# A decayed linear attention with experts: keys decayed in place on VectorE, values copied by ScalarE, TensorE's attention loop written out

## The chip, the cores and the metric

The kernel is one program on one core of a Trainium2 chip. The metric is the device time of a launch in microseconds; lower is better. Engines are called TensorE (PE in the profile), VectorE (DVE), ScalarE (ACT), GpSimd (POOL) and SyncE (SP, which here only issues DMAs).

## What is computed

x is (2, 2048, 128) in f32. It is normalised over its last axis, and the result feeds a chunked linear attention with forget gates (16 heads of 8) and a mixture of 8 experts of which expert 0 and one routed one act on each token. The sum of x and both is the output.

```python
q = silu(x @ Wq.T); k = silu(x @ Wk.T); v = x @ Wv.T
log_f = log_sigmoid(x @ Wf.T + delta)          # cumulated in a chunk: lb
def step(S, inputs):                           # one chunk, per head
    qb, kb, vb, lb = inputs
    o_inter = einsum('bhid,bhde->bhie', qb * exp(lb)[..., None], S)
    A = einsum('bhid,bhjd->bhij', qb, kb) * exp(where(mask, lb_i - lb_j, -inf))
    o_intra = einsum('bhij,bhjd->bhid', A, vb)
    kd = kb * exp(tot - lb)                    # the decayed keys
    S_new = exp(tot) * S + einsum('bhjd,bhje->bhde', kd, vb)
    return S_new, o_inter + o_intra
o = rms_norm(o) * norm_weight;  attention = o @ Wo.T
out = x + attention + sum_e gate_e * (silu(xn @ W1[e].T) * (xn @ W3[e].T)) @ W2[e].T
```

## The kernel before

The program is written by hand: each engine has its own instruction stream, in the order of the source, and semaphores (S[...]) tie them. The stages are: normalisation, projections (which leave the queries qT, the keys k2 with tokens on partitions, and the values v_sb in SBUF), the attention, expert 0 over all tokens, then 22 blocks of routed tokens. An accumulating DMA at the end of each block adds them to the output.

The attention goes over 32 chunks of 128 tokens, alternating between the two batch rows, so chunk n has buffer b = n % 2. It works in subchunks of 64 tokens. For chunk n the engines do this:

- GpSimd: qblk, the queries spread into masked blocks (L517, after the scores of chunk n-2); kd, the keys times the decays sdec (L520); the values copied into the block-shaped vblk (L525, after the attention product of chunk n-2); q_dec of chunk n-1, queries times their growth (L511); and an indirect DMA that scatters 128 normalised rows for the experts (L469).
- TensorE, in `step` (all matmuls are recorded at L983, in the helper mm): 16 matmuls for the scores 32*64 by 32x256; 4 for the state update from kd and vblk (64*128 by 64x128, L1105-1109); the second half of the exponents (118*128 by 118x512); output projection and sum of squares of chunk n-2; then, after VectorE's L896 has read the update, 4 matmuls state times q_dec and 64 of the attention product of chunk n-1; then the first half of the exponents of chunk n+1. Of 16 pairs of chunks the first four are written out, the next eight run in two passes of a loop over four pairs (attend_four), and the last four are written out again.
- ScalarE: copy of the output oT of chunk n-2 (L659), exponential of the first half (L654), square (L666), exponential of the second half (L654), result row of n-2 (L672), and for n = 2 to 18 the high part of one weight tile (L640).
- VectorE: for n = 3 to 19 the low part of one weight tile (L781), then the masked update (L896), decays times scores in two halves (L887), and two state updates (L904, L910).
- SyncE: for each chunk the transposed keys from HBM, the exponents, the growth rows (after L511 of the chunk n-2 frees the buffer), and at some chunks a 512 KB weight tile.

Ahead of the loop VectorE and ScalarE wait for all stores of the transposed keys (k_out), since their first buffers lie where those were. vblk is zeroed once by GpSimd (L498, semaphore blocks_zero).

Of the kernel before, what the change touches and what calls it, by code (L numbers as in the profile page):

```python
# [22 lines left out]
ALU = mybir.AluOpType  # L23
ACT = mybir.ActivationFunctionType
# [98 lines left out]
def build(nc, x, wqkv, wo, wrf, delta, nw, w13, w2, const, dleft, dright, out,  # L123
          k_scr, lb_scr, elb_scr, xsort):
    dleft, dright = dleft.bitcast(BF16), dright.bitcast(BF16)
    with ExitStack() as ctx:  # L126
# [128 lines left out]
        qblk = C.take([P, 2, HQ, P])  # L255
        k_now = C.take([P, 2, P])
        vblk = C.take([P, 2, HQ, HQ * (QR + HD)])
        kd = C.take([P, 2, D])
        q_dec = C.take([P, 2, P])
        ebuf = C.take([P, 2, H * SUB // 2])  # L260
        elb_now = C.take([P, 2, P])
# [193 lines left out]
        def _(pool):  # L455
# [58 lines left out]
            for n in range(NCH):  # L514
                b, c = n % 2, chunk(n // 2, n % 2)
                wait(pool, S["pe_a"], n - 1)
                pool.tensor_tensor(qblk[:, b], qT[:, c * P:(c + 1) * P].unsqueeze(1).broadcast_to([P, HQ, P]),  # L517
                                   cc("hsel").unsqueeze(2).broadcast_to([P, HQ, P]), ALU.mult).then_inc(S["pool_qb"], 1)
                wait(pool, S["pe_u"], n - 1)
                pool.tensor_tensor(kd[:, b, :].rearrange("p (h d) -> p h d", d=HD),  # L520
                                   k2[:, c, :].rearrange("p (h d) -> p h d", d=HD),
                                   sdec[:, c, :].unsqueeze(2).broadcast_to([P, H, HD]), ALU.mult
                                   ).then_inc(S["pool_kd"], 1)
                wait(pool, S["pe_av"], n - 1)
                pool.tensor_copy(v_of(slice(0, P), b), v_sb[:, c, :].rearrange("p (q h e) -> p q h e", q=HQ, h=HQ)  # L525
                                 ).then_inc(S["pool_v"], 1)
                if n:
                    grown_queries(n - 1)
                scatter(EARLY + n)
# [27 lines left out]
        def _(act):  # L557
# [85 lines left out]
            def attend(i):  # L643
                for b in range(2):
                    n = 2 * i + b
                    known = isinstance(n, int)

                    def has(k):
                        return not known or 0 <= n - k < NCH

                    def decays(half):
                        act.wait_ge(S["pe_d"], 2 * n + half + 1)
                        wait(act, S["dve_p"], 2 * n + half - 1)
                        act.activation(ebuf[:, half, :], PS[:, 0, :], ACT.Exp).then_inc(S["act_e"], 1)  # L654

                    if has(2):
                        act.wait_ge(S["pe_av"], n - 1)
                        wait(act, S["pe_w"], n - 3)
                        act.activation(oT[:, b, :].rearrange("p (s i) -> p s i", s=NS), PS[:, 5:7, 0:SUB], ACT.Copy  # L659
                                       ).then_inc(S["act_ot"], 1)  # L660
                    if has(0):
                        decays(0)
                    if has(2):
                        act.wait_ge(S["act_ot"], n - 1)
                        wait(act, S["pe_ss"], n - 3)
                        act.activation(squares[:, b, :], oT[:, b, :], ACT.Square).then_inc(S["act_sq"], 1)  # L666
                    if has(0):
                        decays(1)
                    if has(2):
                        act.wait_ge(S["pe_ss"], n - 1)  # L670
                        act.wait_ge(S[f"scattered{b}"], 16 * (i - 1) + 16)
                        act.activation(rows[:, bass.ds(chunk(i, b, 2), 1), 0:D + 1].rearrange("p o d -> p (o d)"),  # L672
                                       PS[:, 7, 0:D + 1], ACT.Copy).then_inc(S["act_attn"], 1)
                    high_w(n)
# [3 lines left out]
                act.wait_ge(S[f"k_out{v}"], 16 * (NGRP // 4))  # L678
            act.wait_ge(S["slots"], 1)
            act.wait_ge(S["blocks_known"], 1)  # L680

            def sorted_hi(n, u):
                act.wait_ge(S["xs_ps"], n + 1)
# [60 lines left out]
        def _(dve):  # L744
# [127 lines left out]
            for v in range(4):  # L872
                dve.wait_ge(S[f"k_out{v}"], 16 * (NGRP // 4))

            def attend(i):
                for b in range(2):
                    n, c = 2 * i + b, chunk(i, b)
# [28 lines left out]
                    if has(1):  # L906
# [2 lines left out]
                        dve.wait_ge(S["dve_s1"], n)  # L909
                        dve.scalar_tensor_tensor(state[:, u, 0, :], state[:, u, 1, :], dec[:, bass.ds(cu * NS + 1, 1)],  # L910
                                                 um[:, u, 1, :], ALU.mult, ALU.add).then_inc(S["dve_s0"], 1)

            for i in range(CPB):
                attend(i)
# [66 lines left out]
        def _(pe):  # L981
# [90 lines left out]
            def step(i, b):  # L1072
# [17 lines left out]
                if has(0):  # L1090
# [8 lines left out]
                                      k_now[rq, b, tok], qblk[rq, b, :, tok])  # L1099
                    last.then_inc(S["pe_a"], 1)  # L1100

                    pe.wait_ge(S["pool_kd"], n + 1)
                    pe.wait_ge(S["pool_v"], n + 1)
                    wait(pe, S["act_ot"], n - 1)
                    for s in range(NS):  # L1105
                        tok = slice(s * SUB, (s + 1) * SUB)
                        last = mm(PS[:, 5 + s, P:2 * P].rearrange("p (q h e) -> p q h e", q=HQ, h=HQ),
                                  kd[tok, b, :], v_of(tok, b))
                    last.then_inc(S["pe_u"], 1)
                    exponents(1)  # L1110
                if has(2):
# [82 lines left out]
                    pe.wait_ge(S["y_sb"], BT * n - BT)  # L1194
                down(N0 + n, u, [w2_sb[:, bass.ds(e - 1, 1), part].rearrange("p o f d -> p (o f) d") for part in range(2)])

            def attend_four(j):
                for k in range(4):
                    attend(4 * j + k)

            loop(pe, CPB // 4 - 1, attend_four)
            attend_four(CPB // 4 - 1)


            pe.wait_ge(S["act_e"], 2 * NCH)
# [79 lines left out]
```

## Time and profile before

| | us |
|---|---|
| runs, median of 3 | 376.96 |
| runs, lowest and highest | 374.95, 378.18 |
| profiled execution | 376.87 |
| its span | 375.1 |

| engine | busy us | share of the span |
|---|---|---|
| TensorE matmul | 328.8 | 88% |
| VectorE | 265.9 | 71% |
| GpSimd | 243.5 | 65% |
| ScalarE | 222.0 | 59% |

The span runs from the first to the last instruction of the profiled execution; about 1.8 us of its time lie outside. A share over the whole span mixes stages with different limits: the attention, from about 68 to 190 us, has to be read by itself. The granted TensorE clock is given as a share of 2.4 GHz, with two levels, 1.0 and 0.5. A busy TensorE is not one at its peak, since matmuls are pipelined.

### The profile page before, as it was taken

Reading aid. Unit: us, or ns where it says so; the run is one execution under the profiler, and the core shown is the slowest. Engines: PE = TensorE matmul, PEld = TensorE weight load, DVE = VectorE, ACT = ScalarE, POOL = GpSimd, SP = SyncE. Lnnn points to the kernel's source line nnn. Section 1 sums busy time; section 2 is a strip of 40 time slices with the busy share of each in tenths; the row PEclk is TensorE's granted clock in tenths of the full one; section 3 lists DMA queues with packets and bytes.
Section 4 is the critical chain, followed back from the end, with each engine's and each line's share of the span. In section 5 each row is a group of like instructions: output and inputs, shape, how many; then the busy total and the mean of one; then the engine's idle time right before and its main releaser. Section 6 shows DMA issues by size and latency. Waiting matters only on the chain.

```text
span 375.1 us, 14237 instructions
## 1 busy us (share of the span) xinstructions
PE 328.8 (88%) x5226; PEld 268.0 (71%) x5226; DVE 265.9 (71%) x577; ACT 222.0 (59%) x474; POOL 243.5 (65%) x292
## 2 busy tenths in 40 slices
PE   0778899599999989999988999999399997999970
PEld 0667765266666657777777999999299996999960
DVE  4973472255999989889837899978267775777740
ACT  1444788444666656555557777666167776777750
POOL 5423041655999989999949999900047776667773
PEclk9999999656999999999999999999699999999996
DMA  8588029411343422122242111111225445344332
GB/s 223 203 278 257 0 83 181 132 37 48 106 125 106 136 65 67 47 68 72 62 147 104 31 34 36 28 42 29 58 30 74 63 61 66 51 61 64 44 37 21
DMA packets 47505, 31.68 MB, mean 84 GB/s; under 512 B 12542, under 2 KB 45182, under 8 KB 47198
## 3 DMA queue, kind: packets, MB, share of 16 engines
q1 hardware_dynamic: 39662, 22.94, 23.3%
q0 software_dynamic: 7504, 7.95, 12.0%
q8 instruction: 35, 0.57, 0.6%
q10 hardware_dynamic: 288, 0.09, 0.1%
q14 instruction: 16, 0.13, 0.1%
HBM read 18.17 MB, written 12.79 MB: 83 GB/s over the span
## 4 chain that ended last, share of the span: by engine, by line
PE 80%; issue 5%; ACT 4%; POOL 4%; DVE 2%; POOLq 0%; DVEq 0%; ACTq 0%
PE PS L983 77%; POOL out L551 4%; PE PS L999 2%; PE PS L1150 1%; ACT C L577 1%; DVE rows L795 1%; ACT F L697 0%; POOLq L126 0%; ACT Z L589 0%; DVE C L887 0%; ACT L697 0%; ACT L628 0%; ACT L611 0%; POOL C L517 0%; ACT C L687 0%
## 5 line engine op out<-in xcount | busy, mean ns | idle before, releaser
L551 POOL DMA_INDIRECT out<-F,ids x44 | 68.3, 1552 | 56.8 <-DVE ids L920 33.9
L983 PE MATMUL PS<-C 64*32 64x64 f32 (+3 forms) x2816 | 88.6, 278 | 4.0 <-issue 3.0
L983 PEld LDWEIGHTS PS<-C 64*32 64x32 f32 (+3 forms) x2816 | 60.7, 123 | 30.9 <-issue 17.7
L930 DVE TENSOR_TENSOR F<-F,PS 128x512 f32<-128x512 f32 x76 | 51.4, 684 | 23.8 <-PE PS L983 14.8
L983 PE MATMUL PS<-C,W 128*128 128x256 f16 (+1 forms) x530 | 63.4, 277 | 3.9 <-DVE C L924 3.7
L697 ACT ACTIVATE F<-PS 128x512 f32<-128x512 f32 x76 | 45.4, 598 | 28.1 <-PE PS L983 21.1
L983 PEld LDWEIGHTS PS<-C,W 128*128 (+1 forms) x530 | 52.2, 100 | 11.6 <-issue 4.7
L654 ACT ACTIVATE C<-PS 128x512 f32<-128x512 f32 x64 | 38.2, 597 | 30.2 <-PE PS L983 23.6
L936 DVE TENSOR_TENSOR F<-F 128x512 f16<-128x512 f32 x76 | 52.4, 707 | 4.4 <-ACT F L702 1.1
L702 ACT ACTIVATE F<-F 128x512 f16<-128x512 f32 x76 | 47.3, 630 | 11.1 <-DVE F L930 8.6
L983 PE MATMUL PS<-xh,W 128*128 (+1 forms) x256 | 44.7, 273 | 1.7 <-DVE F L930 1.3
L887 DVE TENSOR_TENSOR C<-C,PS 128x512 f32<-128x512 f32 x64 | 41.4, 679 | 0.5
L517 POOL TENSOR_TENSOR C<-Z,kept_cst 128x512 f32<-128x512 f32 x32 | 33.7, 1053 | 10.8 <-ACT sdec L630 10.0
L469 POOL DMA_INDIRECT xsort<-rows,slot_i x32 | 36.0, 1126 | 5.2 <-issue 5.2
L983 PE MATMUL PS<-xl,W 128*128 (+1 forms) x128 | 34.9, 273 | 0.0
L896 DVE TENSOR_TENSOR C<-PS,kept_cst 128x256 f32<-128x256 f32 x32 | 13.4, 420 | 30.1 <-PE PS L983 30.1
L983 PE MATMUL PS<-Z,F 128*128 x528 | 33.7, 219 | 1.0 <-ACT F L711 1.0
L983 PEld LDWEIGHTS PS<-Z,F 128*128 128x128 f16 x528 | 31.5, 98 | 2.1 <-issue 1.3
L983 PE MATMUL PS<-dR,dL 118*128 118x512 bf16 x64 | 27.0, 422 | 4.3 <-ACT dec L632 3.4
L983 PEld LDWEIGHTS PS<-xh,W 128*128 128x128 f16 x256 | 25.0, 98 | 4.8 <-ACT F L697 1.5
L539 POOL TENSOR_SCALAR rows<-rows,small 128x128 f32<-128x128 f32 x32 | 25.3, 790 | 0.1
L659 ACT ACTIVATE C<-PS 128x128 f32<-128x128 f32 x32 | 8.9, 278 | 27.4 <-PE PS L983 27.4
(130 smaller groups left out, 569.7 us busy)
## 6 DMA issues: line engine op xcount, KB each, us to landing
F<-w SPq DMA_DIRECT2D x8, 512.0 KB
xsort<-C POOLq DMA_DIRECT2D x1, 2860.0 KB, 8.8
C<-xsort SPq DMA_DIRECT2D x22, 130.0 KB
x_sb<-x SPq DMA_DIRECT2D x8, 256.0 KB, 4.7
k_scr<-C SPq DMA_DIRECT2D x8, 256.0 KB, 2.5
C<-k_scr SPq DMA_DIRECT2D x32, 64.0 KB, 2.2
C<-elb_scr SPq DMA_DIRECT2D x32, 64.0 KB, 2.1
out<-x_sb SPq DMA_DIRECT2D x16, 128.0 KB, 1.8
```

What stands on the lines that cost most here:

```text
L469: pool.indirect_dma_start(xsort, bass.IndirectOffsetOnAxis(ap=slot_i[:, c:c + 1], axis=0), rows[:, c, :], None).then_inc(S[f"scattered{b}" ...
L517: pool.tensor_tensor(qblk[:, b], qT[:, c * P:(c + 1) * P].unsqueeze(1).broadcast_to([P, HQ, P]), cc("hsel").unsqueeze(2).broadcast_to([P, ...
L539: pool.tensor_scalar(attn[:, c, :], attn[:, c, :], rstd[:, c:c + 1], None, ALU.mult).then_inc(S["pool_attn"], 1)
L551: pool.indirect_dma_start(out, bass.IndirectOffsetOnAxis(ap=ids[:, k:k + 1], axis=0), ysb[:, n % 2, t, :], None, compute_op=ALU.add).then_ ...
L654: act.activation(ebuf[:, half, :], PS[:, 0, :], ACT.Exp).then_inc(S["act_e"], 1)
L697: act.activation(silu[:, half, :], PS[:, 2 + 4 * half, :], ACT.Silu, scale=1.0 / WS).then_inc(S["f_silu"], 1)
L702: act.activation(hid_hi[:, u, 2 * half:2 * half + 2, :].rearrange("p f t -> p (f t)"), silu[:, half, :], ACT.Copy).then_inc(S["f_hi"], 1)
L887: dve.tensor_tensor(pbuf[:, b, half * 512:(half + 1) * 512].rearrange("p (q x) -> p q x", q=2), ebuf[:, half, :].rearrange("p (q x) -> p q ...
L896: dve.tensor_tensor(um[:, b].rearrange("p s (h e) -> p s h e", e=HD), PS[:, 5:7, P:2 * P].rearrange("p s (h e) -> p s h e", e=HD), cc("hma ...
L930: dve.tensor_tensor(silu[:, half, :], silu[:, half, :], PS[:, 3 + 4 * half, :], ALU.mult).then_inc(S["f_h"], 1)
L936: dve.tensor_tensor(hid_lo[:, u, blocks, :].rearrange("p f t -> p (f t)"), silu[:, half, :], hid_hi[:, u, blocks, :].rearrange("p f t -> p ...
L983: return pe.matmul(out_, lhsT, rhs, start=start, stop=stop)
```

## The change

kd as a buffer and both GpSimd operations go. VectorE multiplies k2 by sdec in place, four chunks in one operation: two such operations ahead of the loop (chunks 0 to 3 of each batch row) and six inside it, behind chunks 2, 5, 10, 13, 18 and 21. ScalarE copies the values of chunk n into vblk, between its copy of oT and the first exponential, and waits once for blocks_zero. TensorE takes the decayed keys from k2 and waits for the new semaphores. Its loop of four pairs is written out, so that all 32 chunks are straight code.

```diff
-        kd = C.take([P, 2, D])
...
@@ gpsimd
                 wait(pool, S["pe_a"], n - 1)
                 pool.tensor_tensor(qblk[:, b], qT[:, c * P:(c + 1) * P].unsqueeze(1).broadcast_to([P, HQ, P]),
                                    cc("hsel").unsqueeze(2).broadcast_to([P, HQ, P]), ALU.mult).then_inc(S["pool_qb"], 1)
-                wait(pool, S["pe_u"], n - 1)
-                pool.tensor_tensor(kd[:, b, :].rearrange("p (h d) -> p h d", d=HD),
-                                   k2[:, c, :].rearrange("p (h d) -> p h d", d=HD),
-                                   sdec[:, c, :].unsqueeze(2).broadcast_to([P, H, HD]), ALU.mult
-                                   ).then_inc(S["pool_kd"], 1)
-                wait(pool, S["pe_av"], n - 1)
-                pool.tensor_copy(v_of(slice(0, P), b), v_sb[:, c, :].rearrange("p (q h e) -> p q h e", q=HQ, h=HQ)
-                                 ).then_inc(S["pool_v"], 1)
@@ scalar, attend
                     if has(0):
+                        wait(act, S["pe_av"], n - 1)
+                        c = bass.ds(chunk(i, b), 1)
+                        act.activation(v_of(slice(0, P), b),
+                                       v_sb[:, c, :].rearrange("p o (q h e) -> p (o q) h e", q=HQ, h=HQ), ACT.Copy
+                                       ).then_inc(S["act_v"], 1)
                         decays(0)
...
+            act.wait_ge(S["blocks_zero"], 1)
@@ vector
+            def decayed_keys(g):
+                rows_ = slice(g * GRP, (g + 1) * GRP)
+                keys = k2[:, rows_, :].rearrange("p c (h d) -> p (c h) d", d=HD)
+                dve.tensor_tensor(keys, keys, sdec[:, rows_, :].rearrange("p c h -> p (c h)").unsqueeze(2)
+                                  .broadcast_to([P, GRP * H, HD]), ALU.mult).then_inc(S["dve_kd"], 1)
+
+            dve.wait_ge(S["sdec"], 1)
+            dve.wait_ge(S["drained"], NPIECE)
+            for b in range(2):
+                decayed_keys(b * NGRP // 2)
...
+                    if n % 8 in (2, 5) and n // 8 + 1 < NGRP // 2:
+                        decayed_keys(n // 8 + 1 + (n % 8 == 5) * (NGRP // 2))
@@ tensor
-                    pe.wait_ge(S["pool_kd"], n + 1)
-                    pe.wait_ge(S["pool_v"], n + 1)
+                    pe.wait_ge(S["dve_kd"], 2 * (i // 4) + b + 1)
+                    pe.wait_ge(S["act_v"], n + 1)
...
-                                  kd[tok, b, :], v_of(tok, b))
+                                  k2[tok, chunk(i, b), :], v_of(tok, b))
...
-            def attend_four(j):
-                for k in range(4):
-                    attend(4 * j + k)
-
-            loop(pe, CPB // 4 - 1, attend_four)
-            attend_four(CPB // 4 - 1)
+            for i in range(CPB):
+                attend(i)
```

## Rows read from the trace of the kernel before

**Rows 1.** Windows, attention: us; busy PE, PEld, DVE, ACT, POOL; clock; DMA; GB/s.

```profile
68.00:92.00 24.00, 22.61 (x326) 13.35 (x326) 10.91 (x23) 8.59 (x20) 16.37 (x26) 0.50 0.25 68
...
96.00:151.00 55.00, 51.40 (x1401) 36.03 (x1402) 52.76 (x88) 34.16 (x88) 51.60 (x75) 1.00 0.37 103
151.00:190.00 39.00, 38.97 (x1046) 28.57 (x1046) 33.65 (x57) 20.77 (x57) 36.76 (x57) 1.00 0.21 60
```

**Rows 2.** GpSimd's timeline, chunk 13: start us, duration us, engine, line, operation.

```profile
121.99 1.05 POOL L517 TENSOR_TENSOR C<-Z,kept_cst 128x512 f32<-128x512 f32 x1
122.99 0.47 POOL L520 TENSOR_TENSOR C<-Z,sdec 128x128 f32<-128x128 f32 x1
123.41 0.28 POOL L525 COPY C<-Z 128x128 f32<-128x128 f32 x1
123.67 0.56 POOL L511 TENSOR_TENSOR C<-Z,C 128x128 f32<-128x128 f32 x1
124.39 1.29 POOL L469 DMA_INDIRECT xsort<-rows,slot_i  x1 [0.16 <-issue]
```

**Rows 3.** VectorE's timeline, from one weight split to the next.

```profile
120.12 0.94 DVE L781 SCALAR_TENSOR_TENSOR W<-F,W 128x512 f16<-128x512 f32 x1
120.99 0.41 DVE L896 TENSOR_TENSOR C<-PS,kept_cst 128x256 f32<-128x256 f32 x1
121.32 1.27 DVE L887 TENSOR_TENSOR C<-C,PS 128x512 f32<-128x512 f32 x2
...
123.84 0.94 DVE L781 SCALAR_TENSOR_TENSOR W<-F,W 128x512 f16<-128x512 f32 x1
```

**Rows 4.** Single lines of VectorE over the span: duration ns min/median/max, first and last start.

```profile
L910 DVE SCALAR_TENSOR_TENSOR C<-C,dec x31: 343/791/794, 77.0 to 191.0; 128x128 f32<-128x128 f32 x31
...
L781 DVE SCALAR_TENSOR_TENSOR W<-F,W x16: 683/939/1197, 82.5 to 143.3; 128x512 f16<-128x512 f32 x16
...
L823 DVE TENSOR_TENSOR W<-W x1: 693/693/693, 46.1 to 46.1; 128x512 f32<-128x512 f32 x1
```

**Rows 5.** Timeline of all engines at 139 us, a split beside L511.

```profile
139.16 0.79 DVE L781 SCALAR_TENSOR_TENSOR W<-F,W 128x512 f16<-128x512 f32 x1
...
139.37 0.89 POOL L511 TENSOR_TENSOR C<-Z,C 128x128 f32<-128x128 f32 x1
```

**Rows 6.** TensorE's timeline: first exponents of chunks 3 and 4, scores of 5.

```profile
83.19 0.61 PE L983 MATMUL PS<-dR,dL 118*128 118x512 bf16 x1
...
88.80 0.61 PE L983 MATMUL PS<-dR,dL 118*128 118x512 bf16 x1
...
93.75 1.24 PE L983 MATMUL PS<-C 32*64 32x256 f32 x20
```

**Rows 7.** TensorE's timeline, chunk 22 to 23, and the scores of 31.

```profile
156.78 0.39 PE L983 MATMUL PS<-dR,dL 118*128 118x512 bf16 x1
...
158.18 0.39 PE L983 MATMUL PS<-dR,dL 118*128 118x512 bf16 x1
...
160.16 0.39 PE L983 MATMUL PS<-dR,dL 118*128 118x512 bf16 x1
...
188.04 1.12 PE L983 MATMUL PS<-C 32*64 32x256 f32 x20
```

**Rows 8.** TensorE's timeline, chunk 16, at the loop's boundary.

```profile
134.92 1.11 PE L983 MATMUL PS<-C 32*64 32x256 f32 x20 [0.35 <-issue]
...
137.62 1.42 PE L983 MATMUL PS<-C 128*128 128x64 f32 x68 [0.93 <-issue]
```

**Rows 9.** ScalarE's timeline in the chunk of rows 7.

```profile
157.20 0.60 ACT L654 ACTIVATE C<-PS 128x512 f32<-128x512 f32 x1
157.70 0.30 ACT L666 ACTIVATE C<-C 128x128 f32<-128x128 f32 x1
```

**Rows 10.** ScalarE's and VectorE's timelines, first operations of the attention.

```profile
69.82 0.60 ACT L654 ACTIVATE C<-PS 128x512 f32<-128x512 f32 x1 [1.93 <-DMA k_scr<-C]
...
71.23 0.42 DVE L896 TENSOR_TENSOR C<-PS,kept_cst 128x256 f32<-128x256 f32 x1 [12.30 <-PE PS L983]
```

## The prediction

> **What bounds the kernel now.** The engine shares come first: TensorE is the busiest, so time is won only where it waits or runs slowly. The change touches the attention stage alone, so next come the windows of that stage [rows 1]. Three regimes show. From 68 to 92 us the granted clock is 0.50, which is the 1.2 GHz level, and TensorE is busy 22.6 of 24 us. From 96 to 151 us the clock is 1.00 (2.4 GHz), TensorE has 3.6 us of gaps, VectorE is busy 52.8 of 55 us and GpSimd 51.6. From 151 to 190 us TensorE is busy all the time, and VectorE has slack.
>
> The GpSimd timeline shows why the middle is slow [rows 2]. From L517 at 121.99 to the end of the scatter at 125.68, where the next L517 follows, are 3.7 us, and the queue is full: L517 to L520 1.00, L520 to L525 0.42, L525 to L511 0.26, L511 with the 0.16 before the scatter about 0.72, the scatter 1.29. The two pieces that the change takes out are worth 0.42 + 0.26 = 0.68 us of each period. VectorE runs at the same period, 120.12 to 123.84 = 3.72 us, with nothing idle [rows 3]. Both are full because they hold each other up. The state update L910 (L904 is the same operation on the other subchunk) takes 343 ns at best and 791 ns as a rule; L781 683 at best and 939 as a rule [rows 4]. At 139.16 L781 starts first, and the GpSimd multiply L511 that starts 0.2 us later takes 0.89 us where it took 0.56 before [rows 2], and ends 0.3 us after the split [rows 5]. So operations of VectorE with two inputs in SBUF and GpSimd's elementwise work exclude each other. The PSUM reader L887 runs beside L517 from 121.99 on and takes 1.27 us for its two halves, as anywhere else [rows 2, 3].
>
> The Trainium skill has this as a rule (GPSIMD Engine Reference, 1. Specifications: the SBUF interfaces are shared with VectorE, with contention where a VectorE instruction has two SBUF inputs). It speaks against this change, as the new key multiply on VectorE is of just that kind; the trace agrees [rows 4, 5]. Taken by itself it would put the whole key multiply on both engines.
>
> What TensorE needs by itself: at half clock a chunk takes 88.80 - 83.19 = 5.61 us [rows 6], at full clock 160.16 - 156.78 = 3.38 us in a chunk without a gap [rows 7]. That is the floor which this change can't lower. From the scores of chunk 5 at 93.75 [rows 6] to those of chunk 31 at 188.04 [rows 7] are 26 periods in 94.29 us, 3.63 each.
>
> **The change part by part.**
>
> *GpSimd loses the key multiply and the value copy.* What is left is 3.7 - 0.68 = 3.0 us [rows 2] with the stretched scatter, less where it isn't stretched, below TensorE's 3.38. GpSimd then waits for the scores of chunk n-2 before L517 (two buffers), and stops being a bound. It also collides less: VectorE's three two-input operations need about 0.27 + 0.27 + 0.62 us by themselves (their best durations less the overlap of neighbours), and the elementwise work facing them falls from 2.3 to 1.6 us a period (L517 and L511 [rows 2]).
>
> *VectorE in a chunk with a weight split (n = 3 to 19).* Unstretched: L896 0.33, the two L887 1.2 [rows 3], L904 and L910 0.54, L781 0.62, together 2.7 us; stretched as now 3.72. At a 3.38 period there are 0.7 us of slack if nothing is stretched, so I expect it to fit.
>
> *Key multiply on VectorE, eight operations of 128x512 f32 in place.* No row shows it. The nearest is L823, the same shape and type, 693 ns [rows 4]; the same number of columns beside GpSimd (L781) goes to 1197 ns. I take 0.62 us of queue time, the 0.69 less what neighbours overlap, and for the upper end 0.9. Two run ahead of the loop, n=2 falls in the half-clock stretch, where VectorE idles over 2 us a chunk (10.9 of 24 us busy [rows 1]), n=5 at its edge, and n=21 where the split is over: nothing each. If that cover were gone they would cost 0.6 each. Those at n=10, 13 and 18 fall in full chunks: 2.7 + 0.6 = 3.3 of 3.38, so 0 if all fits and 0.9 each if all is stretched. I take 0.3 each: 0.9 us.
>
> *Value copy on ScalarE, 32 of 128x128.* ScalarE's own SBUF to SBUF operation of that size is 0.30 us [rows 9], so 32 x 0.30 = 9.6 us on an engine that is 34.2 of 55 us busy. Its wait for pe_av is the one that the copy of oT ahead of it already has. It stands in front of the first decay exponential, though, which starts at 157.20 and ends at 157.80, while TensorE needs it for its second exponent matmul at 158.18 [rows 7, 9]: slack 0.38 us against a delay of at most 0.30. Behind that exponential wait the square and the second exponential, whose own releaser is that later matmul. So nothing on the path, with 0.08 us to spare. The blocks themselves are ready about 0.6 us after oT, when TensorE is still at the scores.
>
> *TensorE's loop written out.* At the middle iteration boundary (chunk 16) there are gaps of 0.35 and 0.93 us [rows 8]. The second is partly a wait, and another shift of the loop would hide some of it; together they are at most 1.3 us. The first and last eight chunks were written out already and show no such gaps, so straight code brings no new ones. This is inside the average of 3.63 and goes with it.
>
> *Start of the loop.* VectorE's and ScalarE's queues wait until 69.8 for the key stores, with the key multiplies and the first copy placed behind that wait [rows 10]. The first multiply ends at 70.4, the second at 71.0, or at 72.0 if L517 of chunk 1, which now follows the first scatter at once, gets in between with its 1.05 us [rows 2]. L896 began at 71.23 [rows 10]. So 0 to 0.75 us late; I take 0.5. The half-clock chunks are TensorE's own and give nothing back.
>
> *Moved waits.* SyncE's load of the growth rows waits for GpSimd's L511 and comes earlier, not later; the loads behind it in that queue too. What follows the attention (FFN, GpSimd's tail) hangs on its end and shifts with it.
>
> **Sum.** 26 periods x 3.40 = 88.4, plus 0.9 for the key multiplies: 89.3 us in place of 94.29, 5.0 saved. Plus 0.5 at the start: 4.5 saved. The profiled execution took 376.87 us, the median of the runs is 376.96, so they are one: 376.87 - 4.5 = 372.4 us.
>
> **The rivals.**
>
> *A. TensorE paces the stage* (above): 372.4. With 3.38 and nothing for start and keys it is 370.5; with 0.75 at the start and 0.9 for each key multiply 374.8, at 3.42.
>
> *B. VectorE stays the bound.* If it still meets GpSimd at the wrong moments, the 15 chunks with a split keep 3.72 and three get 0.7 for the keys. Left are the 1.3 us of loop gaps and 11 late chunks at 3.44 (from the scores of chunk 22, 0.3 us after its first exponents at 156.78, to 188.04: 9 periods in 30.9 us [rows 7]) less 3.40: -1.3 - 0.4 + 2.1 + 0.5 = +0.9, so 377.8. For it: VectorE is 96% busy there and gets 5 us of new work. Against: over half of L904 and L910 is waiting for work that goes.
>
> *C. The value copy delays the exponentials.* Slower: if strided writes make it 0.6 instead of 0.30, decay, second exponent matmul and so every full-clock chunk are 0.2 to 0.3 us later than in A: 26 x 0.25 = 6.5, so 378.9. It decides above a delay of 0.38 us. Against it stands the 0.30 us of the square [rows 9].
>
> *D. The clock rises at another chunk.* The trace doesn't show what ended the 1.2 GHz stretch; TensorE was as busy before as after. Each chunk more or fewer at that level is 5.6 - 3.4 = 2.2 us. The start moves, so the rise may. Two chunks earlier: 368.0; two later: 376.8. The Trainium skill (TensorE: Matmul & The Clock Gate, Part 1) says that sustained matmuls bring the full clock and that the moment differs between runs. This trace, with 24 us at 0.50 at 94% busy, shows that sustained work alone didn't suffice.
>
> **How the numbers follow.** A 0.52, B 0.20, C 0.08, D early 0.12, D late 0.08. A by itself would be 370.5 to 374.8. For 8 in 10 the range takes in D early to 368 and B with most of D late: 367.8 to 377.8. About 1% is what a measurement here can tell from no change; the bounds are 373.2 and 380.7. Faster: 0.40 of A and D early, 0.52. Same: the rest of A, nearly all of B, most of D late and a third of C, 0.39. Slower: 0.09.
>
> **What would show it.** Right: GpSimd idle before L517, waiting for TensorE; L904 and L910 back near 0.35 in most full-clock chunks; chunk period 3.4 us between chunks 6 and 31; VectorE idle before L896 also where L781 runs; the gaps at chunk 16 gone. B would show VectorE without idle time and L781 at 0.94 still. C would show ScalarE's first exponential more than 0.4 us after its exponent matmul's end, and TensorE waiting for it. D shows in the granted clock by itself. Wrong for a reason I have not named would be gaps in TensorE's written-out stretch that end with no releaser.

## The result, and the profile after

The changed kernel takes 448.58 us (median of 4, 446.79 to 450.22) against 377.57 (374.95 to 379.17): ratio 1.189, interval 1.180 to 1.198. It was forecast at 372.4, in a range of 367.8 to 377.8. The profiled execution took 449.71 us, with a span of 447.9.

Windows of the attention after (columns as in [rows 1]; the stage now lasts until 267 us):

```profile
69.50:92.00 22.50, 19.27 (x298) 11.67 (x298) 14.34 (x24) 7.90 (x20) 13.34 (x17) 0.50 0.21 62
96.00:151.00 55.00, 53.51 (x850) 35.73 (x850) 30.39 (x58) 23.34 (x64) 26.58 (x27) 0.50 0.26 75
151.00:190.00 39.00, 37.80 (x633) 25.47 (x633) 22.08 (x41) 15.62 (x43) 19.14 (x20) 0.50 0.15 43
190.00:267.00 77.00, 74.66 (x1208) 50.65 (x1208) 31.49 (x61) 26.04 (x77) 25.98 (x32) 0.50 0.19 58
```

The granted clock is 0.50 in all four, the 1.2 GHz level; before it was that only in the first [rows 1]. In 55 us TensorE issues 850 matmuls where it issued 1401. VectorE and GpSimd, full before, are now busy 30.4 and 26.6 of 55 us. The clock records of the trace give one stretch at 0.50, from 69.5 to 267.4 us; before it was 68.0 to 91.9.

Timeline of one chunk after (start, duration, idle before and its releaser in brackets):

```profile
92.72 0.61 PE L993 MATMUL PS<-dR,dL 118*128 118x512 bf16 x1
...
93.44 0.28 ACT L650 ACTIVATE C<-PS 128x128 f32<-128x128 f32 x1 [2.34 <-PE PS L993]
...
94.58 1.03 POOL L516 TENSOR_TENSOR C<-Z,kept_cst 128x512 f32<-128x512 f32 x1 [1.21 <-PE PS L993]
...
96.19 2.19 PE L993 MATMUL PS<-C 128*128 128x64 f32 x67
...
97.37 0.46 POOL L510 TENSOR_TENSOR C<-Z,C 128x128 f32<-128x128 f32 x1 [1.76 <-PE PS L993]
97.89 0.68 DVE L778 SCALAR_TENSOR_TENSOR W<-F,W 128x512 f16<-128x512 f32 x1
97.98 1.46 POOL L468 DMA_INDIRECT xsort<-rows,slot_i  x1 [0.16 <-issue]
98.55 0.30 PE L993 MATMUL PS<-C 64*32 64x64 f32 x1 [0.17 <-issue]
98.78 0.61 PE L993 MATMUL PS<-dR,dL 118*128 118x512 bf16 x1
```

The same stretch before, also at clock 0.50; its next operation, the first exponents at 83.19, is in [rows 6]:

```profile
81.05 2.21 PE L983 MATMUL PS<-C 128*128 128x64 f32 x68
...
83.33 0.29 POOL L525 COPY C<-Z 128x128 f32<-128x128 f32 x1 [2.29 <-PE PS L983]
83.58 0.45 POOL L511 TENSOR_TENSOR C<-Z,C 128x128 f32<-128x128 f32 x1
83.73 1.89 PE L983 MATMUL PS<-C 32*64 32x256 f32 x20
...
84.19 1.02 POOL L469 DMA_INDIRECT xsort<-rows,slot_i  x1 [0.16 <-issue]
```

Before, the value copy L525 waits 2.29 us for the attention product (the group of 68), then follow the growth multiply and, at 84.19, the scatter, about 0.9 us behind the product's end. Over the whole trace this wait shows before only 5 of the 32 copies (8.5 us together): four up to 93.6 us, in and just behind the half-clock start, and one at 139.1. Before the others GpSimd doesn't wait for TensorE: its own queue brings it there late enough. After, there is no copy. The growth multiply L510 waits only for the product's first four matmuls (state times q_dec), and the scatter starts at 97.98, inside the product. The product then stands as 67 matmuls and one more at 98.55: its last is held about 0.48 us, with no releaser that the profile shows. From the exponents at 92.72 to those at 98.78 the period is 6.06 us; before it was 5.61 [rows 6]. So it goes in the first 29 products; in the last three, where no scatter runs any more, no matmul is held.

The hold isn't the stretch of the scatter beside the weight split L778. In a late chunk without a split the scatter takes 1.00 us and the last matmul is as late after its start (0.58 us against 0.57):

```profile
231.57 1.00 POOL L468 DMA_INDIRECT xsort<-rows,slot_i  x1 [0.16 <-issue]
...
232.15 0.30 PE L993 MATMUL PS<-C 64*32 64x64 f32 x1 [0.18 <-issue]
...
232.38 0.61 PE L993 MATMUL PS<-dR,dL 118*128 118x512 bf16 x1
...
233.10 0.28 ACT L650 ACTIVATE C<-PS 128x128 f32<-128x128 f32 x1 [2.87 <-PE PS L993]
```

The last row shows more. ScalarE's copy of the product began at 83.30 before, 0.1 us after the next exponents' start; here it begins 0.7 us after them, 1.53 us after the scatter's start. So the completion, the semaphore signal by which TensorE tells that a matmul is done, is late too. Counted over 72 to 190 us, in bins of 0.1 us from the scatter's start, the semaphore signals that TensorE's matmuls give are:

```
0.0 to 0.1, 0.1 to 0.2, ... us after the start of a scatter
before           8  2 13  8  8 19 11  6  1  0  0  0  0  0 20  3  0  0
after            0  0  0  0  0  0  1  0  0  0  0  1  1  0  3 33  0  0
keys on VectorE  8  3  1  7  2 24 10  0  1  1  0  0  0  0 40 24  1  0
```

None or nearly none comes between 0.9 and 1.4 us, and then many at once. VectorE and ScalarE signal in that time (before: 13 and 23 signals between 0.9 and 1.4; and 24 of VectorE between 1.3 and 1.4 in the run below that waits for the update).

**Where the 71 us came from.** From the start of the first product to that of the last, the attention took 116.7 us before (75.42 to 192.16) and 185.4 after (77.88 to 263.32), 68.7 more, and it began 2.5 later; the span grew by 72.8. Of the 68.7, some 29 holds of 0.47 make 13.6. The other 55 are chunks at the 1.2 GHz level which before ran at 2.4: 28 x (5.61 - 3.63) = 55 [rows 6, 7].

### The profile page after: what moved, and what is told of

Same layout as the page of the kernel before. It is cut to its first block, busy times and chain, and to the rows that moved or that the text cites. A ratio compares the mean times of both kernels' runs of the same rounds, so it can differ in the third digit from the quotient of the medians.

```text
span 447.9 us, 14141 instructions
## 1 busy us (share of the span) xinstructions
PE 398.5 (89%) x5226; PEld 310.7 (69%) x5226; DVE 263.2 (59%) x585; ACT 228.1 (51%) x506; POOL 223.9 (50%) x228
## 4 chain that ended last, share of the span: by engine, by line
PE 81%; issue 4%; ACT 4%; POOL 2%; DVE 2%; DMA 2%; POOLq 0%; SPq 0%; ACTq 0%; DVEq 0%
PE PS L993 79%; POOL out L542 2%; DMA k_scr<-C 2%; PE PS L1009 2%; PE PS L1160 1%; ACT C L568 1%; DVE rows L792 1%; ACT F L694 1%; DVE Z L875 0%; ACT F L699 0%; POOLq L126 0%; ACT Z L580 0%; DVE F L940 0%; ACT L694 0%; ACT L602 0%
## 5 line engine op out<-in xcount | busy, mean ns | idle before, releaser
L993 PE MATMUL PS<-C 64*32 64x64 f32 (+2 forms) x2688 | 116.1, 382 | 5.7 <-issue 4.8
L993 PEld LDWEIGHTS PS<-C 64*32 64x32 f32 (+2 forms) x2688 | 75.0, 167 | 30.5 <-issue 25.4
L904 DVE TENSOR_TENSOR C<-PS,kept_cst 128x256 f32<-128x256 f32 x32 | 13.6, 425 | 85.9 <-PE PS L993 85.9
L516 POOL TENSOR_TENSOR C<-Z,kept_cst 128x512 f32<-128x512 f32 x32 | 33.1, 1034 | 48.5 <-PE PS L993 38.4
L993 PE MATMUL PS<-xh,W 128*128 (+1 forms) x256 | 45.6, 276 | 1.7 <-DVE F L940 1.3
L895 DVE TENSOR_TENSOR C<-C,PS 128x512 f32<-128x512 f32 x64 | 43.7, 683 | 4.5
L468 POOL DMA_INDIRECT xsort<-rows,slot_i x32 | 40.4, 1264 | 4.9 <-issue 4.9
L510 POOL TENSOR_TENSOR C<-Z,C 128x128 f32<-128x128 f32 x32 | 14.9, 464 | 55.5 <-PE PS L993 54.0
L993 PE MATMUL PS<-dR,dL 118*128 118x512 bf16 x64 | 38.7, 605 | 4.2 <-ACT dec L623 3.4
L993 PEld LDWEIGHTS PS<-C,Z 64*128 64x128 f32 x128 | 16.2, 308 | 26.0 <-issue 23.4
```

The costliest lines, as they stand in the source:

```text
L468: pool.indirect_dma_start(xsort, bass.IndirectOffsetOnAxis(ap=slot_i[:, c:c + 1], axis=0), rows[:, c, :], None).then_inc(S[f"scattered{b}" ...
L510: pool.tensor_tensor(q_dec[:, b, :], qT[:, c * P:(c + 1) * P], elb_now[:, b, :], ALU.mult).then_inc(S["pool_qd"], 1)
L895: dve.tensor_tensor(pbuf[:, b, half * 512:(half + 1) * 512].rearrange("p (q x) -> p q x", q=2), ebuf[:, half, :].rearrange("p (q x) -> p q ...
L904: dve.tensor_tensor(um[:, b].rearrange("p s (h e) -> p s h e", e=HD), PS[:, 5:7, P:2 * P].rearrange("p s (h e) -> p s h e", e=HD), cc("hma ...
L993: return pe.matmul(out_, lhsT, rhs, start=start, stop=stop)
```

## The experiments

**One part at a time.** First the kernel before with TensorE's attention loop written out and nothing else (`loop(pe, ...)` becomes `for i in range(CPB): attend(i)`).

> The kernel before with TensorE's attention loop written out and nothing else. Theory S (in the changed kernel GpSimd's scatter starts inside TensorE's attention product, TensorE's last matmul of the product is held for about 0.48 us in each chunk, and the longer chunk of 6.07 us keeps the clock at the 1.2 GHz level for the whole attention): the scatter stays behind the product, so about 375 to 377 us, clock back to 1.0 after some 24 us of attention. Rival U (the written-out stretch itself keeps the clock low or holds the matmul): about 440 to 450 us, with the clock at 0.5 to the end of the attention.

375.43 us, ratio 0.998 (0.993 to 1.003): no change that can be measured.

Then the kernel before with only the value copy moved to ScalarE; the key multiply stays on GpSimd:

```
-                wait(pool, S["pe_av"], n - 1)
-                pool.tensor_copy(v_of(slice(0, P), b), v_sb[:, c, :]...).then_inc(S["pool_v"], 1)
+                        wait(act, S["pe_av"], n - 1)
+                        act.activation(v_of(slice(0, P), b), v_sb[:, c, :]..., ACT.Copy).then_inc(S["act_v"], 1)
```

> The kernel before with only the value copy moved to ScalarE; keys still on GpSimd, TensorE's loop as before. GpSimd's wait for the attention product of chunk n-2 goes with the copy. Theory S: the scatter moves into the product, the hold of about 0.48 us a chunk appears, and the clock stays low: 440 to 455 us. Rival K (the keys on VectorE, or TensorE reading them from their new place, cause it): 370 to 378 us. Rival U: as before, about 377.

444.89 us, ratio 1.176. Its timeline is that of the changed kernel, though GpSimd still has its key multiply, and its clock stays at 0.50 for 187.7 us:

```profile
100.43 2.19 PE L986 MATMUL PS<-C 128*128 128x64 f32 x67
...
102.22 1.47 POOL L469 DMA_INDIRECT xsort<-rows,slot_i  x1 [0.15 <-issue]
102.80 0.30 PE L986 MATMUL PS<-C 64*32 64x64 f32 x1 [0.17 <-issue]
```

And the other half: keys on VectorE, TensorE written out, the value copy left on GpSimd.

> The changed kernel with the value copy left on GpSimd behind its wait for the attention product; keys on VectorE, TensorE's loop written out. Theory S: the scatter stays behind the product, no hold, the clock rises within the attention, and GpSimd has 0.42 us less a chunk: 370 to 376 us. Rival K: 440 to 450 us with a hold. Rival U: 440 to 450.

387.81 us, ratio 1.025 (1.014 to 1.036). The products are not held in turn (0.5 us once, in chunk 12) and the clock is back after 13.7 us, yet the period late in the stage is 4.24 us, where the kernel before has 3.44:

```profile
168.22 1.03 POOL L468 DMA_INDIRECT xsort<-rows,slot_i  x1 [0.16 <-issue]
...
169.67 0.42 DVE L901 TENSOR_TENSOR C<-PS,kept_cst 128x256 f32<-128x256 f32 x1 [2.19 <-PE PS L990]
...
169.71 0.60 ACT L648 ACTIVATE C<-PS 128x512 f32<-128x512 f32 x1 [1.27 <-PE PS L990]
...
170.20 1.42 PE L990 MATMUL PS<-C 128*128 128x64 f32 x68 [0.89 <-issue]
```

The scatter starts with the update matmuls; the masked update L901 gets them only 1.45 us later, at the same moment as ScalarE its exponents, and the product starts 0.89 us late. In the kernel before, at 172.01 us, the scatter starts 0.17 us behind the second exponents (171.84), here 0.36 us ahead of them (168.58). So the key multiply's going, too, moves the scatter to a worse place. (The changed kernel with TensorE's loop kept as a loop was not tried.)

**Is it the scatter?** The changed kernel without its scatters:

> The changed kernel without the 32 scatters of the attention stage and the waits on them; nothing else. Left out: the normalised rows don't reach the routed blocks, which then work on the zero rows that initialise the table, so the contribution of the seven routed experts is missing; their blocks run as before. Theory S (GpSimd's indirect DMA, once it runs beside TensorE's attention product, holds TensorE): no hold in any chunk, half-clock chunks of 5.6 us for about 24 us, then the full clock and chunks of 3.4 us: 365 to 372 us. Rival M (the hold comes from something else that the moved value copy brings beside the product, such as the blocks written by ScalarE or VectorE's operations): the hold of 0.48 us stays, 440 to 450 us.

372.11 us, ratio 0.985 (0.974 to 0.995). The two exponents of consecutive chunks:

```profile
151.14 0.39 PE L989 MATMUL PS<-dR,dL 118*128 118x512 bf16 x1
...
152.30 1.04 POOL L514 TENSOR_TENSOR C<-Z,kept_cst 128x512 f32<-128x512 f32 x1 [1.34 <-PE PS L989]
...
154.49 0.39 PE L989 MATMUL PS<-dR,dL 118*128 118x512 bf16 x1
```

3.35 us a chunk without a gap, and GpSimd waits for TensorE. So it is in most of the stage. In its middle the clock fell to the half level once more, for 10.2 us from 114.9, with TensorE busy 8.2 of the 10 us before, as the profile's row of 40 slices shows (the 6 and 7 in the middle of the attention):

```profile
PEclk9999999669996799999999999999589999999995
```

With the scatters in but as plain writes (`pool.dma_start(xsort[c * P:(c + 1) * P, :], rows[:, c, :])` at the same place):

> The changed kernel with each indirect scatter replaced by a plain write of the same rows and bytes, from GpSimd's queue at the same place, in the order of the tokens (the sort by expert is left out). Theory (what holds the product is the indirect operation, whose addresses GpSimd works out in its 1.46 us): no hold, GpSimd is done with the write in under 0.3 us, and the time is that of the kernel without scatters, 368 to 376 us, or a little above. Rival (any transfer started there, or its 66 KB of writes, holds TensorE's last matmul): holds of 0.48 us in each product at half clock and 440 to 450 us.

370.0 us, ratio 0.983 (0.977 to 0.989). Durations of the write in ns (minimum, median, maximum):

```profile
L468 POOL DMA_DIRECT2D xsort<-rows x32: 569/569/602, 68.6 to 176.8; - x32
```

The same bytes, started at the same place in the queue, cost nothing: period 3.35 us, half clock 13.7 us, no matmul held in most chunks. It is the indirect form; whether by what GpSimd does for it or by the places it writes to was not separated. The kernel before without its scatters:

> The kernel before without its 32 scatters (the routed experts' contribution is left out). Theory: in the kernel before little of the scatter lies on the path, since GpSimd's next product starts late by its 1.3 us but VectorE sets the period: 365 to 374 us, and no fewer than 1 us of it from the attention. Rival (the scatter costs the kernel before nothing): 375 to 378 us.

371.41 us, ratio 0.990 (0.982 to 0.998). So even before, the scatter cost some 4 us (1 to 7 by the interval), be it by TensorE's completions or by the 1.3 us that it takes of GpSimd's full queue.

**Where the scatter stands.** Ahead of the growth multiply (its line moved above `if n: grown_queries(n - 1)`):

> The changed kernel, with GpSimd's scatter of chunk n put ahead of its growth multiply of chunk n-1, nothing else. Theory S: the scatter now starts some 1.2 us before the attention product, the hold is gone or sits elsewhere; if it is gone, chunks take 5.6 us and the clock rises: 368 to 376 us. If the order of these two has nothing to do with the hold, or the hold does not decide over the clock: 440 to 450 us.

389.61 us, ratio 1.030 (1.014 to 1.045).

```profile
150.89 1.23 PE L993 MATMUL PS<-C 128*128 128x64 f32 x46
151.24 1.00 POOL L468 DMA_INDIRECT xsort<-rows,slot_i  x1 [0.15 <-issue]
...
152.54 0.48 PE L993 MATMUL PS<-C 64*32 64x64 f32 x22 [0.41 <-issue]
```

At half clock this order holds nothing, and the clock comes back after 23.9 us, as before. At full clock the product is cut in the middle, by about 0.6 us in 25 products, with a period of 4.06; the clock stays at 1.00. Next, `wait(pool, S["pe_av"], n - 1)` ahead of the scatter, the wait that went with the value copy:

> The changed kernel with one more wait on GpSimd: the scatter of chunk n starts only when the attention product of chunk n-2 is done, as the removed copy had enforced it, but now at once behind it and not 0.7 us later. Theory S: the time in which a scatter keeps TensorE's completions back (0.6 to 1.4 us after its start) then falls on the scores and ends about when the update's completion is due: no hold in the product, the clock rises after some 24 us, full-clock chunks of 3.4 to 3.6 us: 370 to 378 us. If any scatter beside TensorE costs the same wherever it is, chunks of 4.1 us or more: 386 us or over.

379.60 us, ratio 1.006 (1.002 to 1.010): this one line takes back 69 of the 71 us. What is left is a period of 3.75, where the held completions are those of the scores and the update. The same line for the first eight chunks only:

> The changed kernel, with GpSimd's wait for the attention product before the scatter put back for the first eight chunks only; from the ninth on the scatter runs beside the product again. Theory (the hold of the product costs much only because it comes while the clock is at half, and the clock's rise is decided in the first chunks): the clock rises about 14 us after the fall, at full clock the hold of 0.6 us in each product costs a period of 4.0 to 4.1 us as with the scatter before the growth multiply, 23 chunks times 0.3 us above the 379.6 us of the kernel that waits throughout, 384 to 394 us, granted clock above 0.95 in the late chunks. Rival (a product broken in each chunk throws the clock back at any time): the clock falls again after the ninth chunk and the time is 425 to 445 us.

421.86 us, ratio 1.119 (1.106 to 1.133), between the two expectations, and both hold a part. Its four executions took 414.6 to 430.6 us, at mean granted clocks of 0.89 to 0.83, so the share at half clock differs between them; the trace is of the shortest. Its clock, in 40 slices of the span, and a chunk late at full clock:

```profile
PEclk9999998598899999965555799999979999999996
```

```profile
144.58 1.29 PE L995 MATMUL PS<-C 128*128 128x64 f32 x67
...
145.78 1.00 POOL L468 DMA_INDIRECT xsort<-rows,slot_i  x1 [0.16 <-issue]
145.80 0.39 PE L995 MATMUL PS<-dR,dL 118*128 118x512 bf16 x1
...
146.12 1.08 PE L995 MATMUL PS<-C 32*64 32x256 f32 x16
...
147.40 0.28 ACT L652 ACTIVATE C<-PS 128x128 f32<-128x128 f32 x1 [1.84 <-remote]
...
147.97 0.49 PE L995 MATMUL PS<-C,Z 64*128 64x128 f32 x4 [0.77 <-ACT C L657]
...
148.50 0.42 DVE L906 TENSOR_TENSOR C<-PS,kept_cst 128x256 f32<-128x256 f32 x1 [1.78 <-PE PS L995]
```

The scatter starts with the product's last matmul, 0.1 us before its end, and ScalarE gets the product's completion 1.6 us after the scatter's start; its copies, the update and VectorE are late in turn. The period is 4.65 at full clock. The clock falls for 6.8 us at 99.3 and comes back; at 177.8 us it falls again, with TensorE busy 23.6 of the 26.8 us before. From then on, as long as scatters run, each product's last matmul is held as in the changed kernel, at 6.07 us a chunk, and the clock stays at 0.50 until the attention ends 54.6 us later. My theory that the clock is decided in the first chunks falls; it can be lost later. The price of 0.6 us a chunk at full clock was too low: I had taken it from another place of the scatter.

**Is the clock the cause or the sequel?** Sixteen matmuls of 128x512 put ahead of the attention, first in the changed kernel, then in the one before:

> The changed kernel with 16 matmuls of 128x512 on operands that are there, into a PSUM bank that nobody reads, in TensorE's wait before the attention (65.2 to 68.8 us), so that this stage may begin at the full clock. Theory C1 (the clock, once full, holds with the held chunks, as it did from chunk 3 on with the scatter put first): holds of 0.6 us a chunk at full clock, periods of 4.1 us, 380 to 386 us. Theory C2 (with the hold TensorE does too little to keep the level): the clock falls again within the attention, 430 to 450 us.

> The kernel before with the same 16 matmuls in TensorE's wait ahead of the attention. Theory C (the half-clock stretch of 24 us there follows the 3.4 us without matmuls, and costs 4 chunks some 2 us each): the attention begins and stays at the full clock, 367 to 371 us. Rival (the mix of matmuls in the attention lets the clock fall by itself at its start): 374 to 378 us, half-clock stretch still there.

449.49 and 376.13 us, ratios 1.190 and 0.997 (0.992 to 1.001). The fall comes later (at 73.0 and 71.3 us) but it comes, and for the changed kernel it lasts as long as ever (194.6 us). From 68 us to the fall TensorE was busy 2.2 of 5.0 and 1.9 of 3.3 us, so the sparse start of the attention seems to bring it; the held products go with its staying.

**A version that beats both.** Block queries made a chunk ahead, and the scatter let go when TensorE has finished something of its chunk, `sem` being the update or the scores:

```
+                if n + 1 < NCH:
+                    query_blocks(n + 1)
                 if n:
                     grown_queries(n - 1)
+                wait(pool, S[sem], n + 1)
                 scatter(EARLY + n)
```

> The changed kernel, with the block queries made one chunk ahead and each scatter issued when TensorE has finished the update of its chunk, which is where it lies beside the attention of the kernel before. Theory (the place of the scatter against the product sets its price, VectorE's and GpSimd's relief is real): period 3.4 to 3.6 us at full clock, no hold of more than 0.2 us in a product, clock back at full within 14 us, 369 to 375 us. Rival (any scatter that overlaps the product holds it, and the kernel before escaped for another reason): a hold of 0.4 to 0.65 us in most products, period about 4.0 us, 387 us or more.

> As the run with the scatter after the update, but the scatter is issued when TensorE has finished the scores of its chunk, about 0.5 to 1 us earlier. Theory (completions of TensorE are not signalled between 0.9 and 1.4 us after a scatter's start): the stretch without completions falls on the end of the update and on what waits for it (VectorE's masked update) or on the first half of the product; the period is between 3.5 and 4.1 us and the time 374 to 390 us. Rival (only the order against the growth multiply matters): the same time as the run with the scatter after the update within 1%.

After the update 376.72 us, ratio 0.998 (0.993 to 1.002), with 0.1 to 0.2 us held in most products and a period of 3.56; after the scores 373.83, ratio 0.988 (0.978 to 0.998), at 3.40. What was left of the loss seemed to lie at the start, so eight scatters were put ahead of the attention (`EARLY = 8`):

> The kernel with the scatter after the scores, with the scatters of chunks 0 to 7 issued before the attention, beside TensorE's projections (the slots are known at 58.6 us from the span's start and GpSimd idles until 69), and none in the attention's first eight chunks. Theory (what costs is a scatter in the first chunks, where it stretches them and the half clock): half clock 13.7 us or less instead of 17.1, chunks 2 to 7 at 3.35 us, 369 to 372.5 us. Rival (the cost comes back as holds of the projections' matmuls, or the clock is not set by the scatters): 373 to 378 us.

377.66 us. Each scatter waits for the one two before it to land, the eighth ends at 75.3 us, and the first product starts at 82.8 instead of 76.4; from there to the last product's start are 109.6 us. With the first key multiplies earlier too it was 376.78, where 368 to 371.5 was expected. Then four ahead, with the keys:

> As the run before it, with four scatters ahead of the attention instead of eight: from the times at which the eight began (59.27, 60.65, 64.64, 67.53 us) four are done at about 68.5 us, before GpSimd's first block queries, while eight kept it until 75.3. Theory (in that run the start was late by GpSimd, not by the scatters as such): first product at 76 to 78 us, half clock 13.7 us, 370 to 373 us. Rival (scatters beside the projections make the half clock long wherever they end): half clock over 17 us and 375 to 378 us.

373.54 us, ratio 0.992 (0.987 to 0.996): first product at 75.8, but 23.9 us at half clock, which I had not expected. The keys alone, on top of the scatter after the scores:

```
+            for b in range(2):
+                decayed_keys(b * NGRP // 2)
             dve.wait_ge(S["dec"], 1)
             for v in range(4):
                 dve.wait_ge(S[f"k_out{v}"], 16 * (NGRP // 4))
```

> The kernel with the scatter after the scores (373.8 us), with VectorE's first two key multiplies ahead of its wait for the keys' writes to DRAM; no scatter ahead of the attention. Theory (with eight scatters ahead the earlier keys brought the first product forward by 1.0 us, 83.80 to 82.83, without a shorter stretch at half clock): 372 to 374 us, in most executions below the kernel before, ratio 0.985 to 0.995. Rival (the gain of the scatter after the scores was the spread of the executions): 375 to 378 us.

373.51 us, ratio 0.992 (0.988 to 0.996): 0.8% below the kernel before. What the earlier keys add to the scatter after the scores (373.83) is not shown. Its windows and one chunk:

```profile
68.80:85.80 17.00, 15.07 (x224) 8.40 (x226) 9.59 (x18) 6.72 (x17) 9.87 (x11) 0.50 0.25 71
96.00:151.00 55.00, 53.21 (x1420) 37.89 (x1420) 49.55 (x95) 36.06 (x105) 39.09 (x46) 1.00 0.38 105
```

```profile
153.26 0.49 PE L998 MATMUL PS<-C,Z 64*128 64x128 f32 x4
...
153.68 1.00 POOL L468 DMA_INDIRECT xsort<-rows,slot_i  x1 [0.81 <-PE PS L998]
...
153.80 0.42 DVE L909 TENSOR_TENSOR C<-PS,kept_cst 128x256 f32<-128x256 f32 x1 [0.18 <-PE PS L998]
...
154.32 1.50 PE L998 MATMUL PS<-C 128*128 128x64 f32 x68
```

The scatter starts 0.42 us behind the update's start: the update's completion still passes, the quiet time falls into the product, whose own completion is due after it, and only 0.1 us of matmuls is held.

## Why the prediction was wrong

- **The step that failed** is "GpSimd loses the key multiply and the value copy". It took the two operations out of the sum, 0.42 and 0.26 us, and nothing for the wait of the second. "GpSimd then waits for the scores of chunk n-2 before L517 ... and stops being a bound" is true (L516 waits 1.21 us above). But the copy's wait for the product was what kept the scatter out of the product at half clock: it is the 2.29 us before L525 in the kernel before. The rows of GpSimd that the prediction used are of chunk 13 [rows 2], where this wait takes no time. The part on moved waits followed SyncE's queue and left out GpSimd's own last operation. The run with the copy alone moved, and the one line that puts the wait back, show this step to be the whole loss but 2 us.
- **Not foreseeable from the rows used** was what a scatter does to TensorE; but its trace showed it. In [rows 2] the scatter was priced only as 1.29 us of GpSimd's time. In the middle of the stage before, no completion came 0.9 to 1.4 us after its start either, and taking it out saves some 4 us. Part of what was read as two full engines holding each other up may have been this; the run takes 1.3 us a chunk of GpSimd's queue away as well, so the two are not told apart.
- **Rival D** named the right quantity with a bound that was no bound: "each chunk more or fewer at that level is 5.6 - 3.4 = 2.2 us" is right (5.61 - 3.35), but two chunks either way was a guess. The trace of before didn't show what ended the stretch, and then the range had to reach to all 32. It was not put beside the question of what could lengthen a half-clock chunk.
- **What a chunk needs** was right: 3.38 was taken as the floor and 3.40 in the sum, 3.35 measured without scatters and 3.40 with them in a better place. Of the 4.5 us forecast as saved, the best version saved 3 (1.6 to 4.4 by the interval), and it has further edits (block queries ahead, waits, earlier keys). That the kernel without scatters came to 372.1 where 372.4 was forecast is in part luck: it lacks work, and its trace holds the 10.2 us at half clock. (The 374.8 of rival A comes to 374.95 by its own terms.) Rival B falls: VectorE is not the bound even when only the scatters are gone from the kernel before (41.9 of 55 us busy).
- **VectorE's durations.** Sources of the kernel after, ns (minimum, median, maximum), against [rows 4]:

```profile
L912 DVE SCALAR_TENSOR_TENSOR C<-C,dec x32: 344/345/1054, 75.2 to 260.5; 128x128 f32<-128x128 f32 x32
...
L918 DVE SCALAR_TENSOR_TENSOR C<-C,dec x31: 350/647/647, 79.6 to 260.8; 128x128 f32<-128x128 f32 x31
...
L778 DVE SCALAR_TENSOR_TENSOR W<-F,W x16: 677/678/679, 86.3 to 176.8; 128x512 f16<-128x512 f32 x16
...
L875 DVE TENSOR_TENSOR Z<-Z,sdec x8: 678/679/2057, 70.5 to 201.1; 128x512 f32<-128x512 f32 x8
...
L655 ACT ACTIVATE C<-Z x32: 301/302/310, 70.5 to 256.5; 128x128 f32<-128x128 f32 x32
```

  Key multiply 0.68 and value copy 0.30 were sized right, and with the copy rival C falls. The split is back at its best, 0.68, at full clock too. The state updates are not. Before, the first (L904) took 0.69 us as a median and the second (L910) 0.79. Here the first (L912) is at 0.35, but the second (L918), beside the growth multiply L510, still takes 0.65. In the fastest version, where GpSimd's block queries meet them, they take 0.57 and 0.54. The contention that the Trainium skill states (GPSIMD Engine Reference, 1. Specifications) is smaller and not gone.
- **The start** was mis-sized: 0 to 0.75 us, taken as 0.5. The first key multiply took 2.06 us instead of 0.6, with the scatter and L516 beside it; TensorE's update waited 1.73 us for it, and VectorE's first masked update came at 73.47, 2.2 us later than in [rows 10].
- **The loop written out** was bounded at 1.3 us and measured at 0.8, with an interval that holds zero. "Straight code brings no new" gaps isn't settled: holds of 0.4 to 1.3 us in chunks 8, 12 or 13 show in ten kernels with it, but not in three others that ran there at full clock (scatter first, scatter after the product, and its first-eight form), and also in the kernel before (0.38 at chunk 12) and without its scatters (1.07 at chunk 8). What makes them stays open.

## What to carry to other kernels

A wait belongs to all that stands behind it in the queue. When an operation leaves an engine, ask of each operation after it when it will now start, and what will be running on the other engines at that moment, above all if it is an indirect DMA on GpSimd. And where a trace shows a slow level of the clock without showing what ended it, the range has to reach to the slow level in the whole stage, with the question of which edit could lengthen a step there.

## What the runs showed of the hardware

- Beside an indirect DMA on GpSimd (1.0 us, 1.46 beside a two-input operation of VectorE) hardly any of TensorE's completions come between about 0.9 and 1.3 us after its start (40 of 1,685 signals in the first 2.2 us, over the 16 traces with such scatters), and its matmuls are held by 0.48 us at half clock and about 0.6 at full clock. Completions due earlier are kept back too in some places and not in others: with the scatter behind the product, those of scores that end 0.5 to 0.6 us after its start come 0.8 us late, and a product that ends 0.1 us after it is signalled 1.5 us late, while with the scatter after the scores those due at 0.3 to 0.8 us come at once (0.01 us after the matmul's end). The place decides the price: the full-clock period is 3.35 us without it, 3.40 if it begins 0.42 us behind the update's start (the run that waits for the scores), 3.56 at 0.79 us (the one that waits for the update), 3.75 behind the product and its next exponents, 4.06 in the middle of the product, 4.24 together with the update, and 4.65 with the product's last matmul. A plain write of the same rows (0.57 us) does none of it. Why is open: the profile names no releaser, and the short hold 0.1 to 0.6 us after the start, at half clock, lies elsewhere than the later one.
- The granted clock can stay at the 1.2 GHz level for 198 us with TensorE busy 189 of 197.6. The Trainium skill (TensorE: Matmul & The Clock Gate, Part 1) lets sustained matmuls bring the full clock; here they did not. The kernels in which it stayed down are those with a held matmul in each half-clock chunk (period 6.07); with the same work and no hold (5.61) it rose after 10 to 24 us. That is a connection seen in 19 kernels; the hold and the longer period were not separated, and why either matters was not found.
- It can fall in the middle of a stage: at full clock for 72 us at 4.65 us a chunk, then down and never up again before the stage's end. Shorter falls, of 3.4 to 10.2 us, came in four traces, with and without scatters: TensorE was busy 7.9 to 8.7 of the 10 us before each. The kernel with plain writes was busy 8.5 of 10 us in the same place (104.9 to 114.9) and kept the full clock.
